# Attention's output projection moved behind the channel sums, and the aggregated values divided on VectorE

## The reference, cut to what matters

```python
# tokenizer: windows of 4 x 4 pixels; the mean of a window asks, its 16 pixels answer
q = _ln(reduce_feats, ...) @ Wq.T
kv = _ln(unf, ...) @ Wkv.T
attn = softmax(einsum('bhpd,bhpnd->bhpn', q * scale, k), axis=-1)   # n = 16 pixels
aggre = einsum('bhpn,bhpnd->bhpd', attn, v)                          # weighted sum, divided by the softmax sum
h = reduce_feats + aggre @ proj_w.T + proj_b
...
# attention over 256 tokens in two chunks of 128, with a state S between them
scores = einsum('bhcd,bhed->bhce', qi, ki) * mask
intra = einsum('bhce,bhed->bhcd', scores, vi)
inter = einsum('bhcd,bhde->bhce', qi * q_dec, S)
S_new = blk * S + einsum('bhcd,bhce->bhde', ki * k_dec, vi)
out = o @ w_proj + b_proj
h = layernorm(h + out)
```

## Time and profile before

| | us |
|---|---|
| median of 3 runs | 2413.96 (2413.16 to 2414.79) |
| the profiled execution, its own time | 2413.36 |
| its span | 2411.6 |
| TensorE busy | 2253.4 (93%) |
| VectorE busy | 1882.0 (78%) |
| ScalarE busy | 1772.0 (73%) |
| GpSimd busy | 1885.6 (78%) |

### The profile page before, as it was taken

How to read it: one execution, slowest core, us unless ns; L and a number is a source line. 1 busy time by engine, 2 the same in 40 slices (tenths; PEclk the granted TensorE clock), 3 DMA queues, 4 the chain that set the end, 5 groups by cost and what they waited for, 6 DMA issues and landing times. The chain is left out here.

```text
span 2411.6 us, 89169 instructions
## 1 busy us (share of the span) xinstructions
PE 2253.4 (93%) x31921; PEld 1015.0 (42%) x31921; DVE 1882.0 (78%) x4131; ACT 1772.0 (73%) x4281; POOL 1885.6 (78%) x2077
## 2 busy tenths in 40 slices
PE   0799999999999999999999999999999977999997
PEld 0344444444444444444444444444444442222222
DVE  5588888888788888888888888888888867777775
ACT  0888888888888888888888888888888734555554
POOL 3599999999999999999999999999999741333333
PEclk9999999999999999999999999999999978999999
DMA  4333333333333333333333333333333100100001
GB/s 84 72 72 72 73 78 76 76 73 72 72 72 72 72 72 72 74 77 76 76 72 72 72 71 72 72 72 72 74 78 76 25 1 5 23 22 22 22 22 27
DMA packets 573777, 147.82 MB, mean 61 GB/s; under 512 B 573504, under 2 KB 573504, under 8 KB 573504
## 3 DMA queue, kind: packets, MB, share of 16 engines
q1 hardware_dynamic: 573504, 143.53, 29.9%
HBM read 135.10 MB, written 8.39 MB: 59 GB/s over the span
## 5 line engine op out<-in xcount | busy, mean ns | idle before, releaser
L600 ACT ACTIVATE xd<-xb 128x512 f32<-128x512 f32 x512 | 586.1, 1178 | 0.0
L885 DVE TENSOR_TENSOR kqs<-ps,qqT 128x512 f32<-128x512 f32 x512 | 352.8, 689 | 286.5 <-PE ps L394 280.0
L389 PE MATMUL ps<-xd,w_ckv 64*64 64x512 f32 x2048 | 551.6, 615 | 7.5 <-ACT sqs L582 5.5
L394 PE MATMUL ps<-xd,w_ckv 64*64 64x512 f32 x2048 | 551.6, 615 | 0.0
L714 POOL TENSOR_TENSOR pv<-vs,aw 128x512 f32<-128x512 f32 x512 | 534.8, 1077 | 0.0
L582 ACT ACTIVATE sqs<-ps 128x512 f32<-128x512 f32 x512 | 307.6, 601 | 196.3 <-PE ps L394 196.2
L772 POOL TENSOR_TENSOR xt<-xb 128x512 f32<-128x512 f32 x256 | 323.5, 1289 | 58.0 <-DMA xb<-in_x_dram 35.1
L896 DVE TENSOR_TENSOR sm<-ps,decay 128x1024 f32<-128x1024 f32 x256 | 301.3, 1219 | 28.7 <-PE ps L473 24.8
L724 POOL TENSOR_TENSOR pv<-pv 128x512 f32<-128x512 f32 x256 | 322.2, 1283 | 0.0
L416 PE MATMUL ps<-w_ckv,xd 64*64 64x64 f32 x16384 | 297.9, 221 | 0.0
L416 PEld LDWEIGHTS ps<-w_ckv,xd 64*64 64x64 f32 x16384 | 263.5, 135 | 49.5 <-issue 34.4
(11 more groups left out here) (225 smaller groups left out, 3910.3 us busy)
## 6 DMA issues: line engine op xcount, KB each, us to landing
xb<-in_x_dram SPq DMA_DIRECT2D x512, 256.0 KB, 4.3
out_dram<-outb SPq DMA_DIRECT2D x128, 64.0 KB, 1.6
w1p<-in_L_ffn_w_dram SPq DMA_DIRECT2D x16, 16.0 KB
w2p<-in_L_ffn_w_dram SPq DMA_DIRECT2D x8, 16.0 KB
b1p<-in_L_ffn_b_dram SPq DMA_DIRECT2D x8, 0.2 KB
b2v<-in_L_ffn_b_dram SPq DMA_DIRECT2D x8, 2.0 KB
sm<-in_L_tok_Wkv_dram SPq DMA_DIRECT2D x4, 16.0 KB, 2.1
w_av<-in_L_attn_w_qkv_dram SPq DMA_DIRECT2D x4, 16.0 KB, 2.2
```

Of the source, the lines that this page charges most:

```text
L389: nc.tensor.matmul(KB[own, :], w_ckv[own, 2 * P + m * C:2 * P + (m + 1) * C], xd[own, j, :], start=True, stop=True)
L394: mm = nc.tensor.matmul(CB[(1 - m) * C:(2 - m) * C, :], w_ckv[own, m * C:(m + 1) * C], xd[own, j, :], start=True, stop=True)
L600: nc.scalar.activation(xd[:, j, :].rearrange("p (b t) -> p b t", b=ST), xb[:, f, :].rearrange("p (b t d) -> p d b t", b=ST, d=ST)[:, j], A ...
L885: V.tensor_tensor(kqs[:, j, :].rearrange("p (b t) -> p b t", b=ST), KB.rearrange("p (b t) -> p b t", b=ST), qqT[:, s, :].unsqueeze(1).to_b ...
```

## The change

In TensorE's step `selected` is one piece again: all four `selv` products, and `keys_free(0)` behind them. `attended` and `state` now stand between that and `keys(0)`, and belong to one unit further back (`there(i, q - 1, 4)`), since they wait one step longer. On VectorE the two operations that take their results, `sblk` and the addition into `LT`, move with them, from the end of a step to behind the transpose of the next. The division of the aggregated values leaves GpSimd (`normalised` is gone) and becomes a VectorE operation between `keys(0)` and `keys(1)`; the sum before it now writes into eight columns per group of bank 4 (`sgr[:, :, 24:32]`) and not into an SBUF tile. ScalarE's squares of `LT` move from before `gather(3, 0)` to behind the copies `vpad` and `htok`, with a tile `l2t` of their own, and ScalarE waits for `agg_done` before it writes into bank 4. There are no new transfers.

```diff
-                    def selected(part):
-
-                        if not there(i, r, 1):
-                            return
-                        last = P // TG - 1
-                        if part == 0:
+                    def selected():
+
+                        if there(i, r, 1):
                             pe.wait_ge(kq_done, done(i, r, 1, ST))
                             pe.wait_ge(qq_done, done(i, r, 0, 1))
...
                             pe.wait_ge(cs_done, done(i, r, 1, ST))
-                        for g in (range(last), (last,))[part]:
-                            mm = nc.tensor.matmul(quarter(B7[g * TG:(g + 1) * TG, :]), selv[:], of_quarter(sqs, g),
-                                                  start=False, stop=True)
-                        if part == 1:
+                            for g in range(P // TG):
+                                mm = nc.tensor.matmul(quarter(B7[g * TG:(g + 1) * TG, :]), selv[:], of_quarter(sqs, g),
+                                                      start=False, stop=True)
                             mm.then_inc(sel_pe, 1)
...
-                        if there(i, q, 4):
-                            pe.wait_ge(oT_done, done(i, q, 4, 1))
-                            pe.wait_ge(h1_done, done(i, q, 5, 1))
+                        if there(i, q - 1, 4):
+                            pe.wait_ge(oT_done, done(i, q - 1, 4, 1))
+                            pe.wait_ge(h1_done, done(i, q - 1, 5, 1))
                             nc.tensor.matmul(LT, oT[:], w_ap[:], start=True, stop=True).then_inc(pr_done, 1)
...
                     scores()
-                    selected(0)
+                    selected()
                     keys_free(0)
-                    selected(1)
+                    attended()
+                    state()
                     keys(0)
...
                     keys(3)
-                    attended()
-                    state()
                     attn_qk()
...  ScalarE
-                    if there(i, q, 5):
-
-                        act.wait_ge(lt_done, done(i, q, 5, 1))
-                        for m in range(2):
-                            ins = squares(LT[:, m * CR:m * CR + C], ssq[:, m:m + 1], l2[:, m * C:(m + 1) * C])
-                        ins.then_inc(ln_sq, 1)
                     gather(3, 0)
...
+                    if there(i, q, 5):
+
+                        act.wait_ge(lt_done, done(i, q, 5, 1))
+                        for m in range(2):
+                            ins = squares(LT[:, m * CR:m * CR + C], ssq[:, m:m + 1], l2t[:, m * C:(m + 1) * C])
+                        ins.then_inc(ln_sq, 1)
...
                     act.wait_ge(turn_done, done(i, r, 1, 1))
+                    act.wait_ge(agg_done, done(i, q, 2, 1))
...  GpSimd
                     attention()
-                    normalised()
                     weighted()
...  VectorE
                         V.transpose(SB, B7).then_inc(turn_done, 1)
+                    if there(i, q - 1, 4):
+                        dve.wait_ge(pr_done, done(i, q - 1, 4, 1))
+                        dve.wait_ge(hb_done, done(i, q - 1, 4, 1))
+                        if e == 1:
+                            dve.wait_ge(s_pe, pairs(i, q - 1, -1))
+                            dve.wait_ge(o_done, done(i, q - 1, 5, 1))
+                            V.tensor_tensor(sblk[:].rearrange("p (j d) -> p j d", d=D),
+                                            B5[:, 3 * P:4 * P].rearrange("p (j d) -> p j d", d=D),
+                                            headmask[:].unsqueeze(2).to_broadcast([P, SL, D]),
+                                            ALU.mult).then_inc(sb_done, 1)
+                        V.tensor_tensor(LT, LT, htok[:, 1 - e, :], ALU.add).then_inc(lt_done, 1)
                     if there(i, q, 2):
 
                         dve.wait_ge(pv_done, done(i, q, 2, 2))
-                        dve.wait_ge(agg_done, done(i, q, 3, 1))
-                        V.tensor_reduce(agg[:], pv[:, 0:8 * P].rearrange("p (n c) -> p c n", c=P), AX,
-                                        ALU.add).then_inc(agg_ch, 1)
+                        dve.wait_ge(turn_done, done(i, r, 1, 1))
+                        V.tensor_reduce(sgr[:, :, TG - D:TG], pv[:, 0:8 * P].rearrange("p (n j d) -> p j d n", j=SL, d=D),
+                                        AX, ALU.add).then_inc(agg_ch, 1)
                     keys(0)
+                    if there(i, q, 2):
+                        dve.wait_ge(agg_ch, done(i, q, 2, 1))
+                        dve.wait_ge(agT_pe, done(i, q, 3, 1))
+                        V.tensor_tensor(aggn[:].rearrange("p (j d) -> p j d", d=D), sgr[:, :, TG - D:TG],
+                                        rden[:, 1 - s, :].unsqueeze(2).to_broadcast([P, SL, D]),
+                                        ALU.mult).then_inc(agg_done, 1)
                     keys(1)
...
-                    if there(i, q, 4):
-                        dve.wait_ge(pr_done, done(i, q, 4, 1))
...
-                        V.tensor_tensor(LT, LT, htok[:, e, :], ALU.add).then_inc(lt_done, 1)
```

More of the change, by code:

```diff
@@ L161, in vit_tower_kernel @@
             l2 = sb1("l2", [P, P])
+            l2t = sb1("l2t", [P, P])
             vs = sb1("vs", [P, 2, N * P])
@@ L177, in vit_tower_kernel @@
             rden = sb1("rden", [P, 2, SL])
-            agg = sb1("agg", [P, P])
             aggn = sb1("aggn", [P, P])
@@ L516, in attended @@
                     def attended():
-                        if there(i, q, 4):
-                            pe.wait_ge(oT_done, done(i, q, 4, 1))
-                            pe.wait_ge(h1_done, done(i, q, 5, 1))
+                        if there(i, q - 1, 4):
+                            pe.wait_ge(oT_done, done(i, q - 1, 4, 1))
+                            pe.wait_ge(h1_done, done(i, q - 1, 5, 1))
                             nc.tensor.matmul(LT, oT[:], w_ap[:], start=True, stop=True).then_inc(pr_done, 1)
                     def state():
-                        if there(i, q, 4) and e == 0:
-                            pe.wait_ge(kd_done, pairs(i, q, -1))
-                            pe.wait_ge(oT_done, done(i, q, 4, 1))
+                        if there(i, q - 1, 4) and e == 1:
+                            pe.wait_ge(kd_done, pairs(i, q - 1, -1))
+                            pe.wait_ge(oT_done, done(i, q - 1, 4, 1))
                             nc.tensor.matmul(B5[:, 3 * P:4 * P], kd[:], vpl[:], start=True,
@@ L753, in keyed @@
                                 nc.gpsimd.tensor_tensor(qdm[:], qT[:, 1 - e, :], qdec[:], ALU.mult).then_inc(qd_done, 1)
-                    def normalised():
-                        if there(i, q, 2):
-                            pool.wait_ge(agg_ch, done(i, q, 2, 1))
-                            pool.wait_ge(agT_pe, done(i, q, 3, 1))
-                            nc.gpsimd.tensor_tensor(aggn[:].rearrange("p (j d) -> p j d", d=D),
-                                                    agg[:].rearrange("p (j d) -> p j d", d=D),
-                                                    rden[:, 1 - s, :].unsqueeze(2).to_broadcast([P, SL, D]),
-                                                    ALU.mult).then_inc(agg_done, 1)
                     if there(i, r, -2):
@@ L969, in step @@
                         assert n[0] == 5
-                    if there(i, q, 4):
-                        dve.wait_ge(pr_done, done(i, q, 4, 1))
-                        dve.wait_ge(hb_done, done(i, q, 4, 1))
-                        if e == 0:
-                            dve.wait_ge(s_pe, pairs(i, q, -1))
-                            dve.wait_ge(o_done, done(i, q, 5, 1))
-                            V.tensor_tensor(sblk[:].rearrange("p (j d) -> p j d", d=D),
-                                            B5[:, 3 * P:4 * P].rearrange("p (j d) -> p j d", d=D),
-                                            headmask[:].unsqueeze(2).to_broadcast([P, SL, D]),
-                                            ALU.mult).then_inc(sb_done, 1)
-                        V.tensor_tensor(LT, LT, htok[:, e, :], ALU.add).then_inc(lt_done, 1)
                 units(dve, step)
```

## The result

The changed kernel takes 2442.4 us (median of 4 runs, 2442.37 to 2442.83) against 2414.4 for the kernel before (4 runs, 2413.16 to 2414.79): ratio 1.0117, 95% interval 1.0100 to 1.0135. The forecast was 2444. The profiled executions have spans of 2440.3 and 2411.6 us.

The account below looks back on a forecast made before the run. A chain of VectorE, TensorE and ScalarE waits was taken as the bound, not TensorE's 98% busy time. 25.8 + 12.8 + 2.5 - 8.6 - 2.2 = 30.3 us gave 2444 us, 1.3% slower; 8-in-10 range 2427 to 2460.

Parts of the forecast that it names:

- The chain: One step's waits: VectorE mask to first kqs, TensorE keys(1), second kqs, keys(2), ScalarE's seven rows; 14.52 us, the whole step.
- TensorE is the bound: Rival: the held selv product is the loss, moving the others costs nothing; 74 us gained, 2340 us; chance 0.07.
- `sblk` and the addition: On VectorE behind the transpose, 0.21 us each, paid in full; cost 25.8 us and 12.8 us.
- The rule of the full records: VectorE's next operation starts only when the pipe is empty; the two would cost 56 us, not 39; time 2461.
- The transpose: On VectorE, probably held by the channel sums; can now overlap the mask, 8.6 us gained, bounds 0 and 11.
- The late mask: In a loop round's last step VectorE's mask starts 1.24 after the scores, not 1.17; 2.2 us gained.
- The sum: VectorE's sum of weighted values, now written into PSUM: 0.02 us a step as fixed cost, 2.5 us.
- rival on the sum: Sum quicker by the output's place, 2416 us, chance 0.06; or slower by output size, 2458 us, chance 0.10.
- The division: On VectorE between first and second kqs, 0.21 us inside 1.56 us of idle time; cost 0, GpSimd gain 0.
- the case without cover: The division on VectorE without the idle time between the two kqs to cover it: 26 us.
- ScalarE: Squares of LT move into its wait for the next queries; new wait for agg_done included, value 0.
- TensorE's part: 0.60 us at the held selv product goes, keys(0) at 3.17 or 3.39, before it is needed; value on the path 0.

Follow-up runs that it names:

- the first experiment: The kernel before with the channel sums in one piece, the wait for the mask behind all four selv products; 2401.05 us, ratio 0.9944.
- the fastest kernel: The kernel before with channel sums in one piece, VectorE's first kqs before the sum, division on VectorE behind the sum, all in SBUF; 2386.69 us.

## Why the prediction was right, step by step

**The chain.** Right, and tested from three sides: the lag of 0.41 between `kqs` and keys(1) has stayed; an operation between transpose and sum is paid in full (23 and 79 us) while one of 0.2 us behind `kqs` is not (0.3 us in the steady steps); and with `kqs` in front of the sum keys(1) comes earlier. "TensorE is the bound" would have given 2340 us; the undivided sums alone gave 13.5 us and not 74.

**`sblk` and the addition.** 0.21 us each were counted, 0.19 to 0.21 are in the rows: 38.6 us forecast, about 36 by the rows and 35.3 averaged over the steps. Each is paid from start to start, and a record's last 0.09 us cost nothing. The rule of the full records, 2461 us, is refuted. The prediction gives that rule without its exception, though: the same section of the Trainium skill says that a next operation that is not held starts earlier, and that is what the rows here show, 0.08 to 0.09 us before the end.

**The transpose.** 0.07 us was taken, the rows have 0.08 to 0.09: 0.092 averaged over the steps, 11.3 us: the upper bound of the forecast, and not 8.6. The reason given (it was held by the channel sums) is borne out by the first experiment.

**The late mask.** 2.2 us was counted. The trace bears it out: in every fourth step the mask started 1.23 to 1.26 after the scores, and now starts at 1.17 to 1.18. Averaged over the 61 steps with `sblk` it went from 1.218 to 1.179: 2.4 us.

**The sum.** 0.02 us was taken; the record is 0.03 longer (1969 against 1940 ns), and from start to start it is 0.02, 2.7 us in all. Neither rival on the sum holds. That the place of the output is the reason is shown only in part: with the sum back in SBUF the steady steps give back 0.9 us, and where the rest comes from stays open.

**The division.** 0 was right, by the measured 2413.8 for it alone. The price named for the case without cover, 26 us, is about right for an input in PSUM (23 us), and far too low for two inputs in SBUF (79 us behind the transpose).

**ScalarE.** 0 was right in the steady steps: the second `sqs` starts with the second `kqs`, as before. There is little room. In steps without `sblk` ScalarE's statistics end 0.08 us before that `sqs`; 0.2 us more in front of `agg_done` shifts it by 0.03 without a cost, 0.8 us more costs 72 us in the steady steps.

**TensorE's part.** 0 was right beside the undivided sums; without them the waits for `sblk` and the second `sqs` cost some 15 us (6 and 9 above). What the undivided sums free was also over-counted: 0.51 us (keys(0) at +2.92 in the first experiment) and not 0.60. In the changed kernel keys(0) starts at +3.37 and +3.59, not at 3.17 and 3.39, which costs nothing, since VectorE takes it at +6.15 and +6.35.

**What is missing: the last steps.** Together the terms of the steady steps were 30.3 us. By the averages above they are 35.3 + 2.7 - 11.3 - 2.4 = 24.3, and 24.2 were measured. The 28.7 us of the span come out only because 5.0 us arise where no new keys are at work. There the addition into `LT` lies on the path, since what follows it is not hidden behind keys. TensorE in these steps, then VectorE and ScalarE in the last of them (scores at 2005.99):

```profile
1992.80 1.73 PE L488 MATMUL ps<-sm,vpad 128*32 128x128 f32 x32 [2.51 <-ACT l2t L570]
...
2011.60 1.94 PE L488 MATMUL ps<-sm,vpad 128*32 128x128 f32 x32 [2.30 <-ACT l2t L570]
```

```profile
2008.22 2.35 DVE L881 TENSOR_TENSOR sm<-ps,decay 128x1024 f32<-128x1024 f32 x2 [1.40 <-PE ps L469]
...
2010.68 0.31 DVE L900 TENSOR_TENSOR ps<-ps,htok 128x144 f32<-128x144 f32 x1
```

```profile
2011.03 0.22 ACT L570 ACTIVATE l2t<-ps 128x64 f32<-128x64 f32 x1 [4.62 <-DVE ps L900]
```

And TensorE before, in the step whose scores start at 1978.26:

```profile
1983.08 1.94 PE L492 MATMUL ps<-sm,vpad 128*32 128x128 f32 x32 [2.74 <-DVE sm L896]
```

attend waits for ScalarE's squares of `LT`, and these for VectorE's addition behind the mask (and the transpose, while there is one). Before, the addition stood at the end of the step before, and attend waited only for the mask: it started 4.2 to 4.9 us behind its scores in the last five steps, and starts 5.6 to 6.3 us behind them in the changed kernel. No version was run that takes this wait alone away, but the runs bear it out: from the 124th scores to the experts it is 72.2 to 75.8 us in all eight kernels with the moved addition, and 68.7 to 70.5 in all six without.

A forecast that had looked at the last steps would have come out some 5 us higher, and the sum of the steady ones 6 us lower (3.3 for the two operations, 2.7 for the transpose). Two misses of opposite sign lie behind a result that is 1.6 us off. The mechanism and the direction were right; that the number is so close is luck.

## What to carry to other kernels

Where two engines pass work back and forth, price a moved instruction by its place: between what it waits for and what waits for it, 0.2 us cost 23 us over this kernel, and one hole further nothing that the steady steps show (0.3 us). The hole covers only so much: 0.8 us in it cost 72. Test parts of a change together as well as alone: the undivided channel sums are worth 13.5 us alone and 28 beside the moved products, and the division on VectorE is worth 0 alone and 14 us beside the earlier `kqs`. Read the filling and draining steps of a pipeline apart from the steady ones; what is hidden in the one is on the path in the other.

## What the runs showed of the hardware

The division on VectorE, 128x128 elements, takes 276 to 286 ns on average with one input in PSUM, and 874 to 876 ns with both in SBUF while GpSimd works on SBUF. It isn't the operation: in the fastest kernel the same division, SBUF by SBUF, falls into GpSimd's gap and takes 292.

```profile
1002.96 0.29 DVE L898 TENSOR_TENSOR aggn<-agg,rden 128x128 f32<-128x128 f32 x1
```

```profile
1003.06 4.24 POOL L709 TENSOR_TENSOR pv<-vs,aw 128x512 f32<-128x512 f32 x4 [0.87 <-issue]
```

It starts 0.10 before GpSimd's first weighting. In the slow case (one operation more in the hole) the VectorE operation starts 0.38 after it, and then waits for its end. The end is what sets it: in the three kernels with such an operation in the hole (that one, the division alone, and the sum in SBUF), it starts inside a weighting and ends 0.14 to 0.15 us behind that weighting's end in every one of 118 steady steps.

The Trainium skill, page "SBUF — State Buffer", section "SBUF: two separate sides", says of a VectorE operation with two SBUF inputs and a GpSimd operation that reads SBUF that whichever starts first gets the shared ports for the whole instruction, and the other blocks. These rows agree where GpSimd is first. Where VectorE is first they show little: in the fastest kernel the first weighting is 0.04 us longer than the other three (1117 against 1076 ns), though VectorE's record runs on for 0.19 us.

This also gives the sum's new place in PSUM a use that the forecast didn't see: it keeps the division at 0.28 us, though here the hole would have covered the longer one too.
